# A feed-forward whose scaled product stays in its PSUM bank: three product banks, one bank less elsewhere, no padded tile

## The reference

```python
def act_quant(x):
    scale = 127.0 / jnp.clip(jnp.max(jnp.abs(x), axis=-1, keepdims=True), 1e-05)
    return jnp.clip(jnp.round(x * scale), -128, 127) / scale
def weight_quant(w):
    scale = 1.0 / jnp.clip(jnp.mean(jnp.abs(w)), 1e-05)
    return jnp.clip(jnp.round(w * scale), -1, 1) / scale
h = act_quant(x) @ weight_quant(w1).T            # (8, 512, 512) to (8, 512, 2048)
h = depthwise_conv1d(h over the 512 tokens, conv_w (2048, 3), pad 1) + conv_b
h = silu(h)
return act_quant(h) @ weight_quant(w2).T         # back to 512 features
```

## Time and profile before

| | |
|---|---|
| time, median of 3 runs | 3316.15 us (3313.43 to 3318.39) |
| the profiled execution | 3314.49 us, span 3312.7 us |
| granted TensorE clock, mean | 0.893 of full speed |
| feed-forward in the span | about 591 to 1163 us |
| L1216 of the eight items starts at | 707.26, 768.18, 830.96, 892.56, 954.89, 1016.50, 1077.65, 1135.58 us |
| ScalarE's wait ahead of these | 9.43, 8.72, 9.63, 9.63, 9.64, 9.63, 9.52, 8.47 us |

### The profile page before, as it was taken

The page is one execution under the profiler, slowest core; times in us unless marked ns, Lnnn a source line. Parts: engine busy times, 40 slices in busy tenths (PEclk is TensorE's granted clock), DMA queues, the critical chain, the costliest instruction groups (busy, mean ns, idle before and its releaser), DMA issues. The chain is left out here.

```text
span 3312.7 us, 44462 instructions
## 1 busy us (share of the span) xinstructions
PE 2574.8 (78%) x14146; PEld 1327.2 (40%) x14147; DVE 1853.1 (56%) x2672; ACT 1203.9 (36%) x1807; POOL 910.4 (27%) x741
## 2 busy tenths in 40 slices
PE   8377777356666658888887509999999999999970
PEld 4244444122232234444444204444444444444430
DVE  4477776789889676676664642223233333332225
ACT  2233333287887655555554421111111111111110
POOL 0010100066776711111111170005055311350017
PEclk9788888678888879999998859999999999999995
DMA  9560000100000020000000361003033211220018
GB/s 217 119 238 8 7 8 5 51 0 1 1 0 0 0 63 9 9 8 8 11 8 14 117 225 42 32 32 108 32 108 103 76 62 50 89 95 32 32 52 274
DMA packets 118043, 194.11 MB, mean 59 GB/s; under 512 B 55264, under 2 KB 55264, under 8 KB 117456
## 3 DMA queue, kind: packets, MB, share of 16 engines
q1 hardware_dynamic: 92607, 102.96, 11.4%
q0 software_dynamic: 25360, 90.21, 8.0%
HBM read 122.65 MB, written 70.48 MB: 58 GB/s over the span
## 5 line engine op out<-in xcount | busy, mean ns | idle before, releaser
L1806 PE MATMUL e_gate_up<-weights,e_x_t 128*128 x3456 | 772.2, 380 | 1.4 <-ACT e_x_t L1860 1.4
L1806 PEld LDWEIGHTS e_gate_up<-weights,e_x_t 128*128 128x128 bf16 x3456 | 332.8, 98 | 377.4 <-issue 5.1
L1893 DVE TENSOR_TENSOR e_mid<-e_gate,e_gate_up 128x512 f32<-128x512 f32 x144 | 98.9, 687 | 645.8 <-ACT e_gate L1866 645.8
L1826 PE MATMUL e_out<-weights,e_mid_t 128*128 x1728 | 384.7, 379 | 1.1 <-DVE e_mid_t L1906 1.1
L1866 ACT ACTIVATE e_gate<-e_gate_up 128x512 f32<-128x512 f32 x144 | 86.0, 597 | 684.6 <-PE e_gate_up L1806 684.6
L559 PE MATMUL a_turn<-a_wo,a_mixed_t 128*128 128x512 bf16 (+1 forms) x1024 | 284.9, 435 | 2.4 <-DVE a_mixed_t L817 1.7
L1826 PEld LDWEIGHTS e_out<-weights,e_mid_t 128*128 128x128 bf16 x1728 | 169.0, 98 | 204.8 <-issue 1.2
L492 POOL TENSOR_TENSOR a_probs<-a_e,a_probs 128x616 bf16<-128x616 f32 x64 | 85.6, 1353 | 516.4 <-ACT a_probs L726 516.4
L1015 POOL TENSOR_TENSOR f_shared<-f_shared 128x512 f32<-128x512 f32 x128 | 181.0, 1415 | 124.4 <-DVE f_shared L1293 124.4
L1085 PE MATMUL f_out<-f_w,hidden 128*128 128x512 f16 x512 | 143.7, 409 | 91.2 <-ACT hidden L1187 90.7
L650 ACT ACTIVATE a_probs_t<-a_flip 77x512 f32<-77x512 f32 (+1 forms) x256 | 192.3, 801 | 53.7 <-PE a_flip L508 53.6
(11 more groups left out here) (239 smaller groups left out, 4279.8 us busy)
## 6 DMA issues: line engine op xcount, KB each, us to landing
raw_weights<-in_w POOLq DMA_DIRECT2D x72, 512.0 KB, 4.0
sorted_x<-a_zero_row POOLq DMA_DIRECT2D x1, 18432.0 KB, 55.9
e_x_rows<-sorted_x SPq DMA_DIRECT2D x72, 256.0 KB, 2.7
sorted_y<-e_y_rows SPq DMA_DIRECT2D x72, 256.0 KB, 2.0
raw_weights<-in_w SPq DMA_DIRECT2D x24, 512.0 KB, 4.0
x<-in_x SPq DMA_DIRECT2D x4, 2048.0 KB, 21.7
out<-x SPq DMA_DIRECT2D x32, 256.0 KB, 4.1
hidden<-in_w_t SPq DMA_DIRECT2D x1, 4096.0 KB, 14.4
```

The lines of the kernel that those rows point to most:

```text
L1806: last = nc.tensor.matmul(gate_up[half][:, part, :], x_t[:, u, a, k, :], plan.weights13[:, bass.ds(expert % 2, 1), b, k, col:col + 512], s ...
L1826: last = nc.tensor.matmul(out[:, :], mid_t[:, a, j, :], plan.weights2[:, bass.ds(expert % 2, 1), b, j, :], start=(j == 0 and a == b == 0), ...
L1893: nc.vector.tensor_tensor(mid[:, half, :], gate[:, half, :], gate_up[half][:, 1, :], ALU.mult).then_inc(mid_made, 1)
```

## The change

- `scale_down` writes its result back into the same PSUM bank; ScalarE's taps and the left tap read it there. `padded` and its two memsets are gone.
- There are three product banks, given by `bank_of`: chunks 0 to 14 in turn, chunk 15 in bank 1. `first(j)` now waits for the left tap of the chunk that last held the bank: `since` is 3 for most, 2 for chunks 15 and 1, 4 for chunks 0 and 2.
- `front` lies in `scales_bank`, with waits between the two uses; the transposes move from steps 8 and 11 to 9 and 12.
- In a step VectorE does the left tap of j first, then `scale_down(j + 2)`. The side taps cover 511 columns.

```diff
@@ -935,18 +935,22 @@
         xq = low_halves(xn[:, :, :])
         xq_t = sb("xq_t", [P, 2, KD, S], BF16)
         down_row = sb("down_row", [P, 2, S])
-        padded = sb("padded", [P, BUF, S + 2])
         tops = sb("tops", [P, 2, S])
         top2 = sb("top2", [P, TPS])
         up2 = sb("up2", [P, TPS])
         down2 = sb("down2", [P, TPS])
         up2_row = sb("up2_row", [P, S])
 
-        product = [pb(f"product{i}", [P, 512]) for i in range(2)]
+        product = [pb(f"product{i}", [P, 512]) for i in range(3)]
         out = [pb(f"out{i}", [P, 512]) for i in range(TPS)]
-        front = pb("front", [P, 2, 512], F16)
-
         scales_bank = pb("scales_bank", [P, 512])
+
+        front = scales_bank[:, :].bitcast(F16).rearrange("p (i n) -> p i n", i=2)
+
+
+        bank_of = [*(j % 3 for j in range(HC - 1)), 1]
+        turns = bank_of * 2
+        since = [next(d for d in range(1, HC) if turns[HC + j - d] == turns[HC + j]) for j in range(HC)]
 
         w2_in = sem("w2_in"); small_in = sem("small_in"); zeroed = sem("zeroed")
         sums_made = sem("sums_made"); sums_ready = sem("sums_ready"); weights_made = sem("weights_made")
@@ -995,8 +999,6 @@
             nc.gpsimd.tensor_copy(ident_16[:, :], core.ident[:, :]).then_inc(zeroed, 1)
             nc.gpsimd.memset(ones_16[:, :], 1.0).then_inc(zeroed, 1)
             nc.gpsimd.memset(minus[:, :], -OFFSET / P).then_inc(zeroed, 1)
-            nc.gpsimd.memset(padded[:, :, 0:1], 0.0).then_inc(zeroed, 1)
-            nc.gpsimd.memset(padded[:, :, S + 1:S + 2], 0.0).then_inc(zeroed, 1)
 
             def iteration(b, parity, has_middle, has_back, has_front):
                 def scale_up(j):
@@ -1012,8 +1014,8 @@
                     scale_up(j + 2)
                     if has_middle:
                         pool.wait_ge(left_added, HC * b + j + 1)
-                        nc.gpsimd.tensor_tensor(y[:, j % BUF, :], y[:, j % BUF, :], side[:, j % BUF, :], ALU.add
-                                                ).then_inc(right_added, 1)
+                        nc.gpsimd.tensor_tensor(y[:, j % BUF, 0:S - 1], y[:, j % BUF, 0:S - 1],
+                                                side[:, j % BUF, 0:S - 1], ALU.add).then_inc(right_added, 1)
 
             iterations(pool, iteration)
 
@@ -1027,6 +1029,8 @@
             def flip(n, pair):
 
                 pe.wait_ge(rounding, TPS * n + 2 * pair + 2)
+                if pair == 0:
+                    pe.wait_ge(row_copied, n + 1)
                 at_least(pe, front_copied, TPS // 2 * n + pair)
                 for i in range(2):
                     for k in range(KD):
@@ -1049,19 +1053,18 @@
             scales_row(0)
             for pair in range(TPS // 2):
                 flip(0, pair)
-            pe.wait_ge(row_copied, 1)
+            pe.wait_ge(front_copied, TPS // 2)
             weight_sums(1)
             pe.wait_ge(weights_made, 2)
             for j in range(HC):
                 last = nc.tensor.matmul(out[0][:, :], ones_16[:, :], w2[:, j, :], start=(j == 0), stop=(j == HC - 1))
             last.then_inc(columns_ready, 1)
-            pe.wait_ge(front_copied, TPS // 2)
 
             def first(b, j, parity):
 
-                at_least(pe, scaled_down, HC * b + j - 1)
+                at_least(pe, left_added, HC * b + j - since[j % HC] + 1)
                 for k in range(KD):
-                    last = nc.tensor.matmul(product[j % 2][:, :], w1[:, k, j % HC * P:(j % HC + 1) * P],
+                    last = nc.tensor.matmul(product[bank_of[j % HC]][:, :], w1[:, k, j % HC * P:(j % HC + 1) * P],
                                             xq_t[:, parity, k, :], start=(k == 0), stop=(k == KD - 1))
                 last.then_inc(product_ready, 1)
 
@@ -1096,13 +1099,13 @@
                         first(b, j + 2, 1 - parity)
                     if has_front and j == 7:
                         scales_row(b + 1)
-                    if has_front and j in (8, 11):
-                        flip(b + 1, j // 11)
+                    if has_front and j in (9, 12):
+                        flip(b + 1, j // 12)
                     second(j - LAG)
 
                 if has_middle:
                     pe.wait_ge(tops_made, b + 1)
-                    at_least(pe, row_copied, b + 1 + has_front)
+                    pe.wait_ge(front_copied, TPS // 2 * (b + 1 + has_front))
                     for i in range(TPS):
                         last = nc.tensor.transpose(scales_bank[:, i * P:(i + 1) * P], tops[:, 0, i * P:(i + 1) * P],
                                                    core.ident[:, :])
@@ -1165,9 +1168,10 @@
 
                 act.wait_ge(scaled_down, HC * b + j + 1)
                 at_least(act, hidden_made, HC * b + j + 1 - BUF)
-                nc.scalar.activation(y[:, j % BUF, :], padded[:, j % BUF, 1:S + 1], ACT.Identity,
+                scaled = product[bank_of[j % HC]]
+                nc.scalar.activation(y[:, j % BUF, :], scaled[:, :], ACT.Identity,
                                      bias=column(conv_b, j % HC), scale=conv_w[:, j % HC, 1:2])
-                nc.scalar.activation(side[:, j % BUF, :], padded[:, j % BUF, 2:S + 2], ACT.Copy,
+                nc.scalar.activation(side[:, j % BUF, 0:S - 1], scaled[:, 1:S], ACT.Copy,
                                      scale=conv_w[:, j % HC, 2:3]).then_inc(taps_made, 1)
 
             taps(0, 0)
@@ -1252,14 +1256,13 @@
             ternary(0, w1_in, w1)
             scales(0)
             ternary(1, w2_in, w2)
-            dve.wait_ge(zeroed, 8)
+            dve.wait_ge(small_in, 32)
 
             def scale_down(b, j, parity):
                 dve.wait_ge(product_ready, HC * b + j + 1)
-                at_least(dve, taps_made, HC * b + j + 1 - BUF)
-                at_least(dve, left_added, HC * b + j + 1 - BUF)
-                nc.vector.tensor_tensor(padded[:, j % BUF, 1:S + 1], product[j % 2][:, :], down_row[:, parity, :],
-                                        ALU.mult).then_inc(scaled_down, 1)
+                bank = product[bank_of[j % HC]]
+                nc.vector.tensor_tensor(bank[:, :], bank[:, :], down_row[:, parity, :], ALU.mult
+                                        ).then_inc(scaled_down, 1)
 
             dve.wait_ge(row_copied, 1)
             scale_down(0, 0, 0)
@@ -1282,17 +1285,17 @@
                         result(nc.vector.tensor_tensor(tops[:, 0, :], tops[:, 0, :], tops[:, 1, :], ALU.max))
 
                 for j in range(HC):
+                    if has_middle:
+                        dve.wait_ge(taps_made, HC * b + j + 1)
+                        nc.vector.scalar_tensor_tensor(y[:, j % BUF, 1:S], product[bank_of[j]][:, 0:S - 1],
+                                                       conv_w[:, j, 0:1], y[:, j % BUF, 1:S], ALU.mult, ALU.add
+                                                       ).then_inc(left_added, 1)
                     if has_middle and j + 2 < HC:
                         scale_down(b, j + 2, parity)
                     elif has_front:
                         if j + 2 == HC:
                             dve.wait_ge(row_copied, b + 2)
                         scale_down(b, j + 2, 1 - parity)
-                    if has_middle:
-                        dve.wait_ge(taps_made, HC * b + j + 1)
-                        nc.vector.scalar_tensor_tensor(y[:, j % BUF, :], padded[:, j % BUF, 0:S],
-                                                       conv_w[:, j, 0:1], y[:, j % BUF, :], ALU.mult, ALU.add
-                                                       ).then_inc(left_added, 1)
                     for g in range(len(GROUPS) - 2):
                         if has_middle and j == GROUPS[g][1] + 2:
                             largest(g)
```

## The result

The changed kernel takes 3357.94 us (median of 4 runs, 3354.27 to 3359.75), the kernel before 3315.8 in the same session: a ratio of 1.0126, 95% interval 1.0108 to 1.0143. It is 42 us slower; 27 were forecast, and the range ended at 3364.

The account below looks back on a forecast made before the run. A pass is ScalarE's body plus VectorE's end. Items 2 to 6 at +5.0 each (+25), item 1 +3, item 0 +1, item 7 about 0: 29, less 2, +27; 3343 us on the median, range 3318 to 3364.

Parts of the forecast that it names:

- all three silu waits: ScalarE's silu in chunks 0, 8 and 12 would wait for TensorE's `second`, queued behind a refill.
- the clock behind reduction 2: TensorE, idle some six us under VectorE's second `hidden` reduction, would do `first(15)` and `second(12)` at half clock.
- E: ScalarE's taps of chunk 12 to VectorE's reduction 2, 3.83 us before; slow left tap and its wait go: -1.13.
- B: ScalarE's taps of chunk 3 to those of chunk 7, 12.62 us before; four cheaper pairs of taps: -0.32.
- F: VectorE's reduction 2 to reduction 3, 10.74 us before; refills wait for left(13): +2.2 at full clock, +3.8 at half, taken.
- A: ScalarE's scales-row copy to taps of chunk 3, 8.29 us before: +0.8 at full clock, up to +2.7; +1.5 taken.
- D: ScalarE's taps of chunk 10 to those of chunk 12, 6.14 us before: -0.16 to +1.3; +0.4 taken.
- C: ScalarE's taps of chunk 7 to those of chunk 10, 8.25 us before, reduction 1 between: +0.74.
- The 2 us taken off for slack: Deduction from the sum of 29 us over all items, for what small slack eats, leaving +27.
- the stretch to the first L1216: Item 0, with no back part and no silu behind TensorE: bare refills less cheaper taps, +1 us.
- The last pass: Item 7, without norms and scales, paced by GpSimd: 0.45 back for some 10 chunks against new waits, about 0.
- The rival that ended faster: Left taps and GpSimd's adds both shorten without their clash: 4 us a pass, 32 less 2, 3286; chance 0.08.

Follow-up runs that it names:

- e8: Changed kernel with `second(j-1)` put ahead of `first(j+2)` in steps 1, 9 and 13 alone; ratio 1.0017 to the kernel before.
- e3: Changed kernel with 20 filler matmuls on TensorE ahead of `first(15)`, under VectorE's second reduction; ratio 1.0070 to the kernel before.
- e5: Changed kernel with VectorE's old order, `scale_down(j+2)` ahead of the left tap of j, save for chunks 15 and 1; ratio 1.0227 to the kernel before.
- e7: Kernel before with third product bank, shared scales and transposes bank, moved flips, 511 columns; padded tile in SBUF, `scale_down` first; ratio 0.9993 to the kernel before.
- e2: Changed kernel with the scaled product back in the padded SBUF tile and banks released by `scale_down`; ratio 1.0025 to the kernel before.
- e9: Changed kernel with `scale_down` first in steps 0 and 8, `second` first in 1 and 9, reduction 2 and next item's `scale_down(1)` later; ratio 0.9983 to before.
- e1: Changed kernel with `second(j-1)` ahead of `first(j+2)` in every step; ratio 1.0132 to the kernel before.

## Why the prediction was right

*The place* was right: all three silu waits, the clock behind reduction 2, the order in which the segments lose and gain. In the third pass E (-1.17 for -1.13), B (-0.35 for -0.32) and F (+3.82 for +3.8) came to 0.04. e8 shows the cause by taking it away: with `second` no longer behind the refill in three steps, 27 of the 33 us go. e3 shows the clock's part, 1.9 of F.

*The size was partly luck.* The pass came to +5.46 for +5.0 because two terms that were too small, A by 0.8 and D by 0.4, met one that was too large, C by 0.5. F varied from +3.5 to +4.1 over passes 2 to 6, and within the third two errors met: VectorE came to left(13) 5.33 after the start of reduction 2, where 5.67 had been taken, and then `scale_down` for chunk 0 of the next item waited 2.06 for its refill, which stood behind `second(12)` at half clock. The forecast did not have that wait.

*A was undersized.* It was written as +0.8 at full clock and up to +2.7 at half, and +1.5 was taken. It measured +2.37 in the pass shown and 10.64 to 11.59 in all of passes 2 to 6 of both runs. The bias matmuls and `second(0)` run at half clock, behind a wait that `first(3)` did not have. Before, it followed `first(2)` at once (the first row); the rows below it are TensorE's of the changed kernel, and its clock is 0.62 in 853 to 855:

```profile
830.71 2.46 PE L1064 MATMUL f_product<-f_xq_t,f_w 128*128 128x512 bf16 x8
...
852.67 1.15 PE L1067 MATMUL f_product<-f_xq_t,f_w 128*128 128x512 bf16 x4 [2.48 <-DVE f_shared L1290]
853.61 1.91 PE L1085 MATMUL f_out<-f_w_sums,f_minus 128*128 128x512 f16 x4
855.32 1.81 PE L1088 MATMUL f_out<-f_w,hidden 128*128 128x512 f16 x4
```

```profile
853.00:855.00 2.00, 2.00 (x8) 0.76 (x7) 1.82 (x4) 1.65 (x3) 2.00 (x2) 0.62 0.00 0
```

With the mean of +2.3 in place of +1.5 five passes would have had 4 us more.

*D* measured 5.89 to 7.57, from -0.2 to +1.4, as the clock happened to stand; +0.4 was taken, +0.8 came on average. *C* was +0.45, not +0.74: the reduction to the instruction behind it is 4.66 (874.10 to 878.76) where the forecast kept the 4.94 of before, of which 0.22 was a wait ahead of `scale_down`. The mean of C is lower still, +0.24, because C of before was 9.43 in pass 2, not 8.25.

*The 2 us taken off for slack* were not there, and the stretch to the first L1216 lost 3, not 1. The first pass lost 2.3 for 3. The last pass is level, as forecast: B went from 12.11 to 9.45, and F (+3.2), A and C took it. e5, which has the old order, has 9.45 there too, and e7, with the same order and the tile in SBUF, 12.08: the gain comes with the product in PSUM.

*Prices.* Taps were 24 and 19 ns shorter by their durations, but their starts moved by 0.04 each, as assumed (C, B). `scale_down` to PSUM costs 9 ns, in bounds. The surcharge of the Trainium skill's page "VectorE: DVE Perf Modes" (section on the TRN2 errata) for PSUM sources did not come: the left tap has a median of 749 with PSUM and a shortest of 737 with SBUF, and not 65 more. Rows after confirm the clash and its end: with one SBUF input no left tap exceeds 752 ns, as the Trainium skill's "SBUF — State Buffer" has it in its section on who interferes with whom. The shorter left tap shows only where VectorE paces: the changed kernel is 1.1 shorter than e2 in C and 0.6 in E.

*The rival that ended faster* failed where it was said to: each exposure costs at least a refill, 1.1 to 2.1 us. e9 hides part of them by its order and ends 6 us below the kernel before, where that rival had 30. Whether another order gives the rest is open.

## What to carry to other kernels

When a buffer's release moves to a later reader, list for each refill what stands between release and next use in every queue, and what stands behind the refill in the producer's queue: here the second list (`second`, and silu through it) made 27 of the 33 us (e8). Put a waiting instruction behind work that is ready, step by step and not in all steps at once; e8's three steps gave 27 us where all steps lost 10 to 13 (e1). TensorE that had stood idle for 5.7 us did a refill on the critical path in 1.89 us and not in 1.04: price such a refill by its cold row.

## What was not expected of the hardware

ScalarE's durations grow while it is not waiting and its pace stays the same: the centre taps of the pass above start at 871.45, 873.82 and 876.18 and last 0.78, 0.79 and 0.79, later 0.82 at 892.88, up to 847 ns in the tile view, and return to 0.76 to 0.78 after a wait. In SBUF they had stayed within 794 to 821. Start to start is the measure there, not the duration. Why a duration grows is open.

Freed of the clash, GpSimd's own additions had a longest of 1298 ns where 1732 stood, so both sides of it gained.
